# A two-block graph network on one core: the opening in another order, and the low halves of the feed-forward weights made by GpSimd in place of VectorE

## What is computed

```python
h = max(layernorm(x), 0)
Wh = h @ W                                    # block 0, once
e = leaky(Wh@a1 [:,None] + Wh@a2 [None,:]); e = where(adj > 0, e, -9e15)
att = softmax(e); att = where(att < 16th largest of its row, 0, att)
x = x + elu(att @ Wh)
h = max(layernorm(x), 0)
for l in range(3):                            # block 1
    s = leaky(h@wi [:,None] + h@wj [None,:] + b); s = where(adj + eye > 0, s, -inf)
    t = layernorm(h + softmax(s) @ h) * g1 + beta1
    h = layernorm(t + gelu(t @ W1[l] + b1) @ W2[l] + b2) * g2 + beta2
x = x + h
```

## Time and profile before

| | |
|---|---|
| runs of the kernel before | 2846.93, 2843.44, 2842.48 us (median 2843.44) |
| span of the profiled execution, first to last instruction | 2840.5 us |
| the profiled execution's own device time | not listed apart from the runs; the median lies 2.94 us above its span |
| busy share of the span | PE 96%, PEld 86%, DVE 81%, ACT 82%, POOL 73% |
| chain that ended last | PE 80%, POOL 5%, issue 5%, DVE 4%, ACT 3%, DMA 2% |
| DMA | 88.63 MB, mean 31 GB/s |

### The profile page before, as it was taken

The page is one execution under the profiler, slowest core; times in us unless marked ns, Lnnn a source line. Parts: engine busy times, 40 slices in busy tenths (PEclk is TensorE's granted clock), DMA queues, the critical chain, the costliest instruction groups (busy, mean ns, idle before and its releaser), DMA issues.

```text
span 2840.5 us, 55392 instructions
## 1 busy us (share of the span) xinstructions
PE 2719.1 (96%) x17764; PEld 2449.2 (86%) x17764; DVE 2293.8 (81%) x7766; ACT 2326.9 (82%) x4806; POOL 2080.0 (73%) x2217
## 2 busy tenths in 40 slices
PE   4698999999999999999999999999999999999995
PEld 4578988999999998998899899999899999888884
DVE  6777888888888888888888888888888888887542
ACT  4577988888888888888888888888888888888763
POOL 0355777877777787787787777778777777877774
PEclk8798999999999999999999999999999999999997
DMA  5000010111011011101101110110111011010001
GB/s 182 25 27 27 29 33 11 32 35 35 27 34 35 9 34 35 35 27 35 35 9 35 35 35 27 35 34 9 35 35 34 27 35 27 19 25 20 11 10 15
DMA packets 96322, 88.63 MB, mean 31 GB/s; under 512 B 9120, under 2 KB 94368, under 8 KB 96032
## 3 DMA queue, kind: packets, MB, share of 16 engines
q1 hardware_dynamic: 79136, 68.32, 7.8%
q0 software_dynamic: 16896, 16.78, 4.6%
HBM read 47.34 MB, written 37.75 MB: 30 GB/s over the span
## 4 chain that ended last, share of the span: by engine, by line
PE 80%; POOL 5%; issue 5%; DVE 4%; ACT 3%; DMA 2%; POOLq 0%; SPq 0%; ACTq 0%; DVEq 0%
PE ps_ff L3065 11%; PE ps_mm L3042 11%; PE ps_mm L3044 11%; PE ps_mm L3043 10%; PE ps_ff L3066 10%; PE ps_ff L3067 10%; PE ps_ag L3100 5%; PE ps_ht L3112 3%; PE ps L3164 2%; DMA out<-H 2%; POOL a_lo L506 2%; PE ps_s L3088 1%; PE ps_s L3078 1%; PE ps L3177 1%; PE ps L3178 1%
## 5 line engine op out<-in xcount | busy, mean ns | idle before, releaser
L3065 PE MATMUL ps_ff<-w_hi,a_hi 128*128 128x256 f32 x3072 | 892.0, 290 | 10.1 <-POOL a_lo L506 5.3
L506 POOL TENSOR_TENSOR a_lo<-A,a_hi 128x512 fp32r<-128x512 f32 x384 | 524.3, 1366 | 486.7 <-ACT a_hi L1077 486.4
L3066 PE MATMUL ps_ff<-w_lo,a_hi 128*128 128x256 f32 x3072 | 855.6, 279 | 0.0
L3067 PE MATMUL ps_ff<-w_hi,a_lo 128*128 128x256 f32 x3072 | 855.0, 278 | 0.0
L1069 ACT ACTIVATE A<-ps_mm,b_col 128x512 f32<-128x512 f32 x768 | 517.3, 685 | 251.7 <-PE ps_ff L3067 147.8
L3042 PE MATMUL ps_mm<-ht_hi,w_hi 128*128 128x512 f32 x1536 | 627.0, 408 | 3.7 <-DVE ht_lo L2327 2.8
L3065 PEld LDWEIGHTS ps_ff<-w_hi,a_hi 128*128 128x128 f32 x3072 | 578.2, 188 | 45.7 <-issue 11.7
L3044 PE MATMUL ps_mm<-ht_lo,w_hi 128*128 128x512 f32 x1536 | 606.5, 395 | 0.0
L3043 PE MATMUL ps_mm<-ht_hi,w_lo 128*128 128x512 f32 x1536 | 604.6, 394 | 0.0
L3066 PEld LDWEIGHTS ps_ff<-w_lo,a_hi 128*128 128x128 f32 x3072 | 579.0, 188 | 12.5
L3067 PEld LDWEIGHTS ps_ff<-w_hi,a_lo 128*128 128x128 f32 x3072 | 579.2, 189 | 0.0
(11 more groups left out here) (120 smaller groups left out, 5315.2 us busy)
## 6 DMA issues: line engine op xcount, KB each, us to landing
xr<-in_x SPq DMA_DIRECT2D x32, 512.0 KB, 4.2
out<-x SPq DMA_DIRECT2D x32, 512.0 KB, 4.8
out<-H POOLq DMA_DIRECT2D x32, 512.0 KB, 6.2
mask_in<-mask_park SPq DMA_DIRECT2D x96, 128.0 KB, 4.1
adj_sb<-in_adj SPq DMA_DIRECT2D x32, 256.0 KB, 4.4
mask_park<-mask_out SPq DMA_DIRECT2D x32, 128.0 KB, 4.0
X<-in_L_gnn_W SPq DMA_DIRECT2D x3, 1024.0 KB, 5.2
H<-in_L_gnn_W SPq DMA_DIRECT2D x3, 1024.0 KB, 7.1
```

What stands on the lines that cost most here:

```text
L506: pool.tensor_tensor(a_lo[:, at], A[:, at], a_hi[:, at].bitcast(F32), ALU.subtract).then_inc(s["a_lo_gpsimd"], 1)
L3065: pe.matmul(out_g, a_hi[:, at, cols], w2_hi[:, l, m], start=first, stop=False, skip_group_check=True)
L3066: pe.matmul(out_g, a_hi[:, at, cols], w2_lo[:, l, m], start=False, stop=False, skip_group_check=True)
L3067: last = pe.matmul(out_g, a_lo[:, at, cols], w2_hi[:, l, m], start=False, stop=final, skip_group_check=True)
```

## The change

`iteration` and `closing` stay as they are on all engines. The change has two parts.

First, the low halves of W1 and W2 go from VectorE to GpSimd. On VectorE `w1_low` was two instructions (scale and subtract in one pass, 128x1024 each) and `w2_low` one of 128x2048. GpSimd scales the staged W1 in place in one instruction of 128x2048 and subtracts in a second, which waits for the first by a new semaphore, and takes one of 128x2048 for W2: nine instructions of 128x2048 for the three layers.

```diff
@@ gpsimd
+            def w2_low(l):
+                pool.wait_ge(s["w2_hi_made"], l + 1)
+                pool.tensor_tensor(w2_lo[:, l], w2_stage, w2_hi[:, l].bitcast(F32), ALU.subtract).then_inc(s["w2_split"], 1)
+
+            def w1_low(l):
+                pool.wait_ge(s["w1_hi_made"], l + 1)
+                pool.wait_ge(s["w1_biased"], l + 1)
+                pool.tensor_tensor(w1_stage, w1_stage, g1_col[:, l].rearrange("p (c o) -> p c o", o=1).to_broadcast([P, DC, HID]),
+                                   ALU.mult).then_inc(s["w1_scaled"], 1)
+                pool.wait_ge(s["w1_scaled"], l + 1)
+                pool.tensor_tensor(w1_lo[:, l], w1_stage, w1_hi[:, l].bitcast(F32), ALU.subtract).then_inc(s["w1_split"], 1)
@@ vector
-            def w1_low(l):
-                dve.wait_ge(s["w1_hi_made"], l + 1)
-                dve.wait_ge(s["w1_biased"], l + 1)
-                for d in range(DC):
-                    last = stt(out=w1_lo[:, l, d], in0=w1_stage[:, d], scalar=g1_col[:, l, d:d + 1],
-                               in1=w1_hi[:, l, d].bitcast(F32), op0=ALU.mult, op1=ALU.subtract)
-                last.then_inc(s["w1_split"], 1)
-
-            def w2_low(l):
-                dve.wait_ge(s["w2_hi_made"], l + 1)
-                tt(w2_lo[:, l], w2_stage, w2_hi[:, l].bitcast(F32), ALU.subtract).then_inc(s["w2_split"], 1)
```

Second, `opening` has another order on every engine, with the same calls but for the moved ones. The start of SyncE's list, as the diff reads when its lines are put in their order:

```diff
-load_w0() load_w1(0) load_x(0) load_a0() load_cols() load_x(1) load_adj(0) load_w2(0) load_rows() load_adj(1) load_wij() load_w1(1)
+load_x(0) load_x(1) load_a0() load_w0() load_cols() load_adj(0) load_wij() load_rows() load_w1(0) park_mask(0) load_mask(0, 0) load_adj(1) load_w2(0) load_w1(1)
```

More of the change, by code:

```diff
@@ L2366, in opening @@
                 z_topk(0)
-                bias_cols(0)
+                masks(1)
+                mix_low(0, 0)
                 z_recip(0)
-                w2_low(1)
-                mix_low(0, 0)
-                w1_low(1)
+                bias_rows()
                 z_out(0, 0)
@@ L2474, in opening @@
                 y1_sum(1, 1, 1)
+                y1_moments(1, 1)
+                elu(3, 0)
+                a_low(2, 0, 1)
                 node_scores(0, 2)
-                y1_moments(1, 1)
-                ht_low(2, 0, 0)
-                mix_low(3, 0)
-                ht_low(2, 0, 1)
+                mix_low(3, 1)
+                e0_scores(4)
                 scores_mask(0, 2)
-                scores_max(0, 2)
-                z_recip(3)
-                z_out(3, 0)
-                recip(0, 2)
@@ L2499, in opening @@
                 y1_sum(0, 2, 1)
                 y1_moments(0, 2)
-                a_low(2, 0, 7)
-                scores_mask(3, 0)
-                scores_max(3, 0)
+                node_scores(3, 0)
                 y_sum(2, 0)
@@ L2506, in opening @@
                 a_low(1, 1, 1)
-                e0_scores(4)
-                a_low(1, 1, 3)
+                ht_low(0, 2, 0)
+                z_mask(4)
+                scores_mask(3, 0)
+                x_moments(5)
+                scores_max(3, 0)
+                ht_low(0, 2, 1)
+                z_max(4)
+                a_low(1, 1, 3)
+                node_scores(2, 1)
+                a_low(1, 1, 5)
+                z_topk(4)
+                a_low(1, 1, 7)
+                scores_mask(2, 1)
@@ L2532, in opening @@
                 node_scores(1, 2)
[L2533 to L2535 removed]
+                ht_low(3, 0, 1)
+                a_low(0, 2, 7)
+                elu(4, 0)
                 scores_mask(1, 2)
[L2537 to L2544 removed]
@@ L2572, in opening @@
+                a_low(2, 1, 7)
                 ht_low(1, 2, 1)
-                node_scores(3, 1)
-                z_mask(5)
-                z_max(5)
-                a_low(2, 1, 7)
+                z_topk(5)
+                y_sum(2, 1)
                 scores_mask(3, 1)
-                y1_sum(4, 0, 1)
+                z_recip(5)
+                a_low(1, 2, 1)
+                y_moments(2, 1)
+                a_low(1, 2, 3)
+                masks(6)
+                mix_low(5, 0)
+                ht_low(4, 0, 0)
@@ L3261, in opening @@
                 mm2(0, 1, 0)
-                turn_p(2, 0)
                 mm2(0, 1, 1)
+                mm2(0, 1, 2)
                 mm1(0, 1, 4)
                 mm1(0, 1, 5)
-                mm2(0, 1, 2)
-                turn_e0(3)
+                turn_z(3)
                 mm2(0, 1, 3)
+                turn_p(2, 0)
+                mm1(0, 1, 6)
                 agg(2, 0, 0)
-                mm1(0, 1, 6)
+                turn_sj(1, 1)
+                z_mix(3, 0)
                 mm1(0, 1, 7)
+                agg(2, 0, 1)
```

1252 lines of the change are left out of this document (618 added, 634 removed).

## The result

The changed kernel took 2892.85 us (2891.65 to 2896.47), the kernel before 2844.03 beside it: a ratio of 1.0174, 95% interval 1.016 to 1.0189, some 49 us slower where 16 faster were forecast. The profiled span is 2889.7 us.

The account below looks back on a forecast made before the run. The prediction looked to TensorE's 75 us of idle time in the first 240 us, dense behind. An 18 us earlier start of (2,0) less 2 us given back made -16 us: median 2827.5 us, range 2809 to 2843.

Parts of the forecast that it names:

- Steps 1 to 9: Opening's chain from group 0's scores to unit (2,0)'s start: new order brings that start to 212 us, -18 us.
- step 7: End of y_moments work y1_moments(1, 0) in the opening: 140.57 us becomes 134.7, -5.9 us.
- Part one: Low halves on GpSimd: nine instructions of 4.55 us, 41 us in all, relieve VectorE of 14.5 us but can block it.
- step 4: node_scores(0, 0) on VectorE: held by w1_low(1) on GpSimd, ends at 68.5 us instead of 63.15, +5.4 us.
- Step 10: Work sent behind unit (2,0)'s start, node_scores(0, 2) and its mask, is late next: 2 us given back.
- The slower case: All nine GpSimd instructions stand on the chain, (2,0) starts at about 239 us: 2852 us, chance 0.14.
- The first rival: GpSimd's lock costs VectorE little in the opening, some 14 us come back: 2813 us, chance 0.14.
- The second rival: Gap ahead of (2,0) doesn't close; VectorE's chain or other work fills freed time: 2839 us, chance 0.16.

Follow-up runs that it names:

- tail_new: Kernel before up to unit (2,0)'s first mm1 on each engine, low halves on VectorE, then the opening's remaining calls in the changed order: 2914.73 us, ratio 1.0249.
- cut_245: Changed kernel's order on each engine up to 245 us of its trace, low halves on GpSimd, then the order before: 2841.13 us, ratio 0.9986.
- head_new: Changed kernel up to unit (2,0)'s first mm1 on each engine, then the opening's remaining calls in the order before: 2845.83 us, ratio 1.0.
- lows_vector: Changed kernel's order on all engines, but the low halves made by VectorE again: 2891.56 us, ratio 1.0166.
- seam_gpsimd: Changed kernel, with only GpSimd's calls behind 500 us put back in the order before: 2860.81 us, ratio 1.0054.
- turn_late: seam_gpsimd with turn_sj of five units three or four calls later in TensorE's list: 2878.02 us, ratio 1.0106.
- short_h_seam: seam_gpsimd with GpSimd's h_scale and h_bias cut to 128x4 from unit (2,0) to group 7, so output differs: 2849.99 us, ratio 1.0019.
- lows_only: Kernel before with its order on all engines, only the low halves moved to GpSimd: 2868.38 us, ratio 1.0085.

## Why the prediction was wrong

**The step that failed** is in its first paragraph: "behind them the engines' lists are the same, and an earlier or later dense stretch moves the end one for one". The lists are the same only from unit (5,0) on (509 us on TensorE), and on GpSimd from 651 us. I took `opening` for the first 240 us because TensorE is dense behind 229.75, though the text of the function runs on for four more groups, also rewritten. That dense stretch was a property of the old order and not of the kernel. tail_new, with nothing but that later part changed, loses 70 us, and "From there on the trace should be as before" is what the trace refuted.

**Steps 1 to 9 held, but for step 7.** Scores of group 0 end at 16.15 (15.8 said), `turn_z(0)` starts at 29.66 (28.5), `r_norm(0)` ends at 58.3 (58.0), `node_scores(0, 0)` at 67.35 (68.5), `y1_moments(0, 0)` at 82.4 (82.4), (0,0)'s part at 123.0 (122), (1,0)'s first `mm1` starts at 148.75 (149), the gap is 6.3 (8), (2,0)'s first `mm1` starts at 213.5 (212). Step 7 is off: `y1_moments(1, 0)` ends at 138.3 where 134.7 was said.

**Part one held.** GpSimd's rows in the changed kernel:

```profile
L551 POOL TENSOR_TENSOR w_lo<-X,w_hi x3: 4598/4617/4628, 33.6 to 89.5; 128x2048 fp32r<-128x2048 f32 x3
L543 POOL TENSOR_TENSOR w_lo<-H,w_hi x3: 4602/5053/5267, 38.2 to 143.9; 128x2048 fp32r<-128x2048 f32 x3
```

4.6 to 5.3 us for the 4.55 taken; the scaling took 3.6 to 3.8, near the prediction's lower bound of 3.7. The Trainium skill ("GPSIMD Engine Reference", "Elementwise — side-by-side cycle accounting") gives 4497 ns for that size, and the trace agrees to some 2% for the shortest. The lock shows where step 4 put it. The first pass of `node_scores(0, 0)` and the GpSimd row that it waits for:

```profile
60.16 4.75 DVE L2274 CUSTOM_DVE_ANT_0 junk<-X,wij_row 128x256 bf16<-128x256 f32 x1
```

```profile
60.03 4.60 POOL L551 TENSOR_TENSOR w_lo<-X,w_hi 128x2048 fp32r<-128x2048 f32 x1
```

**Step 10 was mis-sized.** The 2 us given back at (2,0) are 10.6 where all behind is in the old order (cut_245: 14.4 us ahead at (2,0), 3.8 at (3,0)); 6.8 of them are waits and 3.8 go with the granted clock of 0.96. The scores of (0,2) end no sooner when TensorE starts something else: `turn_sj(0, 2)` starts at 223.65 us in the kernel before, 223.52 in head_new and 230.14 in cut_245. So even without the later part the first 240 us were worth 3 us, or 10 with the low halves on VectorE, not 16.

**The rivals.** The slower case came, but not by its mechanism: (2,0) did not start at 239, and lows_vector shows that the low halves were not the loss. One figure of that rival was misread: idle times of 35.5 and 20.9 us would by their length hold twelve rows of 4.55 us, not five or six. The first rival, a cheap lock, falls by the pass of 4.75 us. The second rival, that another wait fills the freed time, is what cut_245 does, inside (2,0) instead of ahead of it.

**What stays open**: why the new order loses time ahead of (5,0). Of the 66 us, 33 are lost from (5,0) to (7,0); they go with GpSimd's list behind 500 us (seam_gpsimd). About 9 are lost from (2,0) to (3,0), where cut_245 loses 10.6 with the old order behind, and 24 from (3,0) to (5,0). For these 33 us ahead of (5,0), VectorE's holding by GpSimd is the best supported cause, with 19 us that went away with 18 of it, but turn_late's time does not follow it, so the cause stays open.

## What to carry to other kernels

Before a stretch is called unchanged, find the last instruction at which each engine's two lists differ, engine by engine; a dense stretch in the old trace says nothing of the new order. A start moved forward is a gain only if what comes behind can keep the pace: look for what the closed gap had waited for, since it will be waited for further on. Where one engine's hand-ordered list overhangs into a loop, its head of the line must not wait for a step that the loop does later.

## What the runs showed that was not expected

Less work on GpSimd made the dense loop slower: in short_h_seam (5,0) to (7,0) takes 172.2 us where seam_gpsimd takes 167.0, although GpSimd has less to do there; 8 us of the 19 gained are lost again by the end (10.8 are left). TensorE's longest wait there is the one of `turn_z` for `z_topk` on VectorE, 5.3 us in five waits from 483 to 910 us, which seam_gpsimd does not have. A possible reading, which no run tests, is that an order tuned to one rhythm of VectorE and GpSimd is not safe against either becoming faster.

The lock itself showed at its longest in the changed kernel, 4.75 us for a pass of 0.42, and in lows_only, 4.70. The Trainium skill ("SBUF — State Buffer", "Who interferes with whom") says that the second to issue waits fully; the trace agrees, with a pass that ends 0.28 us behind GpSimd's instruction of 4.60.
